# Experts' weights repeated by a transfer from memory and multiplied in by GpSimd, up sums in two banks

## The reference

```python
shared_out = _silu_and_mul(xf @ shared_w1.T) @ shared_w2.T
probs = jax.nn.softmax(xf @ gate_w.T, axis=-1)
routing_weights, selected = jax.lax.top_k(probs, TOP_K)
combine = zeros((T, E)).at[arange(T)[:, None], selected].add(routing_weights)
act = _silu_and_mul(gate_up)                 # silu(gate) * up, each expert's units
moe_out = jnp.einsum('te,tei,ehi->th', combine, act, w2)
return moe_out + shared_out
```

## Time and profile before

| | us |
|---|---|
| median of 3 runs | 1206.95 (1202.5 to 1208.85) |
| the profiled execution, its device time | 1210.45 |
| its span, first to last instruction | 1208.7 |
| TensorE busy with matmuls | 1041.3 |
| VectorE busy | 789.5 |
| ScalarE busy | 575.7 |
| GpSimd busy | 388.5 |
| TensorE's mean granted clock | 0.944 |

### The profile page before, as it was taken

One profiled execution on the slowest core, in us unless ns is written; L12 is line 12 of the kernel. 1 busy time (PEld: TensorE's weight loads), 2 busy tenths in 40 slices (PEclk: granted clock), 3 DMA queues, 4 the chain that ended last, 5 costly groups with the idle time before them and its releaser, 6 DMA issues. The chain is left out here.

```text
span 1208.7 us, 19206 instructions
## 1 busy us (share of the span) xinstructions
PE 1041.3 (86%) x6554; PEld 783.9 (65%) x6554; DVE 789.5 (65%) x1651; ACT 575.7 (48%) x1129; POOL 388.5 (32%) x423
## 2 busy tenths in 40 slices
PE   3699878999877898859999875799999889999998
PEld 3456536888766677736665454566655578888887
DVE  6367756577865466748888676677776365656655
ACT  3578753443433244306567542146555634444443
POOL 5312213355402244331211232222111044555553
PEclk9899979899998899969999997699999999999999
DMA  7957611342320127564550244937250122333332
GB/s 200 253 117 162 141 48 57 94 144 82 96 79 1 42 83 168 152 140 111 141 114 21 61 105 116 196 64 168 84 90 21 40 65 76 104 101 101 105 106 85
DMA packets 72762, 124.98 MB, mean 103 GB/s; under 512 B 9453, under 2 KB 41478, under 8 KB 70250
## 3 DMA queue, kind: packets, MB, share of 16 engines
q1 hardware_dynamic: 63274, 90.49, 24.6%
q0 software_dynamic: 9408, 33.45, 15.9%
HBM read 94.15 MB, written 30.80 MB: 103 GB/s over the span
## 5 line engine op out<-in xcount | busy, mean ns | idle before, releaser
L2008 DVE TENSOR_TENSOR ff_hl<-ff_h,ff_hh 128x512 fp32r<-128x512 f32 x114 | 135.4, 1188 | 154.2 <-ACT ff_hh L1894 153.8
L606 PE MATMUL psum<-ff_xh,ff_wh 128*128 128x512 f32 x424 | 175.9, 415 | 25.2 <-POOL ff_wl L1953 16.5
L1953 POOL TENSOR_TENSOR ff_wl<-ff_raw,ff_wh 128x512 fp32r<-128x512 f32 x92 | 119.8, 1302 | 236.7 <-ACT ff_wh L1905 236.7
L1050 ACT ACTIVATE probs<-psum 128x512 f32<-128x512 f32 x256 | 144.6, 597 | 85.1 <-PE psum L866 81.2
L1918 ACT ACTIVATE ff_s<-psum 128x512 f32<-128x512 f32 x98 | 58.6, 598 | 257.7 <-PE psum L606 248.2
L866 PE MATMUL psum<-queries,keys 128*128 128x512 f32 x384 | 156.9, 440 | 13.1 <-DMA keys<-keys_out 4.9
L606 PE MATMUL psum<-ff_xh,ff_wl 128*128 128x512 f32 x392 | 157.3, 401 | 0.0
L875 PE MATMUL psum<-keys,queries 128*128 128x512 f32 x256 | 118.4, 479 | 25.2 <-DMA queries<-queries_out 9.5
L606 PE MATMUL psum<-ff_wh,ff_hh 128*128 128x256 f32 x456 | 131.0, 291 | 9.2 <-DVE ff_hl L2008 9.2
L606 PE MATMUL psum<-ff_wh,ff_hl 128*128 128x256 f32 x456 | 130.1, 289 | 0.0
L899 PE MATMUL psum<-probs,values 128*32 128x256 f32 x1664 | 113.0, 394 | 2.0 <-DVE probs L1444 1.9
(11 more groups left out here) (268 smaller groups left out, 2194.0 us busy)
## 6 DMA issues: line engine op xcount, KB each, us to landing
ff_raw<-in_ff SPq DMA_DIRECT2D x92, 320.0 KB, 3.0
keys_out<-keys_turned SPq DMA_DIRECT2D x36, 512.0 KB, 4.2
keys<-keys_out POOLq DMA_DIRECT2D x48, 384.0 KB, 7.8
ff_raw<-in_ff SPq DMA_DIRECT2D x106, 128.0 KB, 2.1
queries_out<-queries_turned SPq DMA_DIRECT2D x36, 256.0 KB, 3.0
queries<-queries_out POOLq DMA_DIRECT2D x32, 256.0 KB, 4.8
w_raw<-in_w SPq DMA_DIRECT2D x12, 256.0 KB, 3.5
queries<-queries_out POOLq DMA_DIRECT2D x16, 192.0 KB, 7.7
```

The costliest lines, as they stand in the source:

```text
L606: last = eng.matmul(dst, lhs[i](k), rhs[j](k), start=start and n == 0, stop=stop and n == groups * len(pairs) - 1, skip_group_check=True)
L1050: ins = eng.activation(dst, src, ACT.Exp, scale=SCALE)
L1953: then(eng.tensor_tensor(ff_wl[:, slot, 0:2 * D], raw(n, slot)[:, 0:2 * D], ff_wh[:, slot, 0:2 * D].bitcast(F32), ALU.subtract), "f_w1r")
L2008: then(eng.tensor_tensor(ff_hl[:, slot, :], ff_h[:, slot, :], ff_hh[:, slot, :].bitcast(F32), ALU.subtract), "f_hr")
```

## The change

The select columns, the `combine` matmul and VectorE's `weighted` go. Instead, ScalarE copies the turned weights (experts by 512 tokens) to `combine` in f32 as one part; SP writes them to memory so that each run of 16 units has its own row (`weights_out`, two transfers for each half), and then loads, for each tile, its 8 rows with each row repeated on 16 partitions (`load_weights`, 256 KB) into a new buffer `ff_w`. GpSimd multiplies `silu(n)` by it (`weighted`), between `lo_up(n+1)` and `lo_down(n)`. VectorE's `gated(n)` multiplies that by the up sum and gives the hidden values at once. The bank set free serves as a second up bank, so that `up(n)` waits for `gated(n-2)`. In layer 1 the shared expert comes first, and its two tiles get a row of ones. ScalarE's order becomes `split_up(n+1)`, `half_hi(n-1)`, `silu(n)`, `split_down(n)`; `split_up(n+1)` waits for `up(n-1)` and handles 512 columns, and the `u` piece is 256 KB.

```diff
+RUN = 16
+RUNS = P // RUN
-GATE_BANKS, UP_BANK, SPREAD_BANK = (5, 6), 7, 4
+GATE_BANKS, UP_BANKS = (5, 6), (7, 4)
...
             def up(n, slot, h):
-                w(eng, "f_td", n)
+                w(eng, "f_hm", n - 1)
...
-            def spread(n, slot, h):
-                w(eng, "f_hm", n)
-                then(eng.matmul(psum[:, SPREAD_BANK, :], ff_wh[:, slot, BS:BS + P], combine[h][:, :], start=True, stop=True),
-                     "f_cf")
...
-                    w(eng, "f_cf", n - 1)
+                    w(eng, "f_uf", n - 1)
                     ins = eng.activation(ff_wh[:, slot, 0:BD], raw(n, slot)[:, 0:BD], ACT.Copy)
...
             def body(n, slot, some, j):
-                if not sign:
-                    silu(n, slot)
                 last = isinstance(n, int) and n == N - 1
                 if not last:
                     split_up(n + 1, 1 - slot, j + slot)
                 half_hi(n - 1, 1 - slot)
+                if not sign:
+                    silu(n, slot)
                 split_down(n, slot, j)
...
+            def weighted(n, slot, j):
+
+                eng.wait_ge(sems[f"d_fw{slot}"], (j + (ff_before(f, f"d_fw{slot}") + 1)) * 16)
+                w(eng, "f_sd", n + 1)
+                then(eng.tensor_tensor(ff_s[:, slot, :], ff_s[:, slot, :], ff_w[:, slot, :], ALU.mult), "f_sw")
...
                 if not (isinstance(n, int) and n == N - 1):
                     lo_up(n + 1, 1 - slot)
+                weighted(n, slot, j)
                 lo_down(n, slot)
...
             def gated(n, slot):
-                w(eng, "f_sd", n + 1)
+                w(eng, "f_sw", n + 1)
                 w(eng, "f_uf", n + 1)
-                then(eng.tensor_tensor(ff_s[:, slot, :], ff_s[:, slot, :], psum[:, UP_BANK, :], ALU.mult), "f_td")
-
-            def weighted(n, slot):
-                w(eng, "f_cf", n + 1)
-                w(eng, "f_td", n + 1)
                 w(eng, "f_hh", n - 1)
-                then(eng.tensor_tensor(ff_h[:, slot, :], ff_s[:, slot, :], psum[:, SPREAD_BANK, :], ALU.mult), "f_hm")
+                then(eng.tensor_tensor(ff_h[:, slot, :], ff_s[:, slot, :], psum[:, UP_BANKS[slot], :], ALU.mult), "f_hm")
...
+        def weights_out(eng, h):
+
+            spec, ends = FFN[f], RUNS * tiles
+            runs = wm[f][h].rearrange("t g c -> (t g) c")
+            e0, each = spec["HS"] // RUN if SHARED_FIRST[f] else 0, spec["H"] // RUN
+            e1 = e0 + spec["E"] * each
+            w(eng, "f_cth", h + 1)
+            src = combine[h][0:spec["E"], :].rearrange("e (one c) -> e one c", one=1)
+            eng.dma_start(runs[e0:e1, :].rearrange("(e g) c -> e g c", g=each),
+                          src.to_broadcast([spec["E"], each, HALF])).then_inc(sems["d_wm"], 16)
+            s0, s1 = (0, e0) if e0 else (e1, ends)
+            src = combine[h][spec["E"]:spec["E"] + 1, :].rearrange("e (one c) -> e one c", one=1)
+            eng.dma_start(runs[s0:s1, :].rearrange("(one g) c -> one g c", one=1),
+                          src.to_broadcast([1, s1 - s0, HALF])).then_inc(sems["d_wm"], 16)
+
+        def load_weights(eng, n, tile, slot, h):
+            w(eng, "f_sw", n - 1)
+            if isinstance(n, int) and SHARED_FIRST[f] and n % tiles < FFN[f]["HS"] // P:
+                eng.dma_start(ff_w[:, slot, :], a["one"].to_broadcast([P, HALF])).then_inc(sems[f"d_fw{slot}"], 16)
+                return
+            src = wm[f][h][bass.ds(tile, 1), :, :].rearrange("one g (r c) -> (one g) r c", r=1)
+            eng.dma_start(ff_w[:, slot, :], src.to_broadcast([RUNS, RUN, HALF])).then_inc(sems[f"d_fw{slot}"], 16)
...
         def sp(eng, first, last):
             def load(n, slot, some, _):
-                load_tile(eng, n, n - tiles * half_of(some), slot)
+                h = half_of(some)
+                load_tile(eng, n, n - tiles * h, slot)
+                if not sign:
+                    load_weights(eng, n, n - tiles * h, slot, h)
...
-            steps(step, max(first, tiles), last)
+            first = max(first, tiles)
+            if first == tiles <= last and not sign:
...
+                n = tiles + ones
+                load_tile(eng, n, ones, n % 2)
+                weights_out(eng, 1)
+                load_tile(eng, n + 1, ones + 1, (n + 1) % 2)
+                eng.wait_ge(sems["d_wm"], weights_written(f, 1))
+                for m in (n, n + 1):
+                    load_weights(eng, m, m - tiles, m % 2, 1)
+                first = n + 2
+            steps(step, first, last)
```

More of the change, by code:

```diff
@@ L368, in __init__ @@
                 else:
-                    self.before[st] = ("f_acc", 4) if ring == FIRST_SUMS else ("f_lo", 2 * KC) if blk == 3 else ("f_ctd", 2)
+                    self.before[st] = ("f_acc", 4) if ring == FIRST_SUMS else ("f_lo", 2 * KC) if blk == 3 else ("f_cth", 2)
                 kind, by = emptied(blk, st)
@@ L475, in flamingo @@
     down_row = at("down_row", OREG + 4096, [P, D])
-    combine = [at(f"combine{i}", (SREG + 8192, OREG + 4096)[i], [P, HALF], F32R) for i in range(2)]
+    combine = [at(f"combine{i}", (SREG + 8192, OREG + 4096)[i], [P, HALF]) for i in range(2)]
     ff_tensors = []
@@ L544, in flamingo @@
     nd = nc.dram_tensor("maxima_out", (B, HALVES, 64, P), F32, kind="Internal").ap()
+    wm = {f: [nc.dram_tensor(f"weights_out{f}{h}", (TILES[f], RUNS, HALF), F32, kind="Internal").ap() for h in range(2)]
+          for f in ROUTED}
     kept = nc.dram_tensor("kept", (KT, P), F32, kind="Internal").ap()
@@ L1087, in do @@
                 elif st[0] == "ce":
-                    ff_parts[blk].weights_hi(eng, 0, plan.bank["ct",])
+                    ff_parts[blk].weights(eng, 0, plan.bank["ct",])
                 if st in between:
@@ L1229, in ln @@
                     eng.wait_ge(sems[f"d_x{b}"], 16)
+                if blk:
+                    ff_wait(eng, blk - 1, "f_acc", QT * (b + 1))
                 for qt in range(QT):
@@ L1643, in clear @@
         def clear(self, eng):
-            eng.memset(combine[0][:, :].bitcast(F32), 0.0)
             eng.memset(rt_w[:, :, self.E:24], -1.0)
@@ L1668, in route @@
             if part == 0:
-                if h:
-                    eng.memset(combine[1][:, :].bitcast(F32), 0.0)
                 self.w(eng, "f_rt", h + 1)
@@ L1704, in turn_weights, with weights @@
             then(last, "f_ct")
-        def weights_hi(self, eng, h, bank):
+        def weights(self, eng, h, bank):
             self.w(eng, "f_ct", h + 1)
             then(eng.activation(combine[h][0:self.EC, :], psum[0:self.EC, bank, :], ACT.Copy), "f_cth")
-        def weights_lo(self, eng, h, bank):
-            EC = self.EC
-            self.w(eng, "f_cth", h + 1)
-            then(eng.tensor_tensor(combine[h][32:32 + EC, :], psum[0:EC, bank, :], combine[h][0:EC, :].bitcast(F32),
-                                   ALU.subtract), "f_ctd")
     ff_parts = [Part(f) for f in range(4)]
@@ L1863, in body @@
                     w(eng, "f_lo", 2 * KC)
-                    w(eng, "f_ctd", 2 if not sign else 0)
                 gate(n, slot, h)
@@ L1874, in body @@
                     up(n, slot, h)
-                    spread(n, slot, h)
             program(eng, body, does)
@@ L1921, in act @@
                     "route": lambda e, h, p: part.exponentials(e, h, B1) if p == 0 else None,
-                    "combine": lambda e, h: part.weights_hi(e, h, B2),
+                    "combine": lambda e, h: part.weights(e, h, B2),
                     "late": lambda e, *name: heads.late(*name), "lead": lambda e, n: lead.lead(n), "mem": lambda e, name: lead(name)}
@@ L2028, in dve @@
                     "route": lambda e, h, p: part.route(e, h, p, B1),
-                    "combine": lambda e, h: part.weights_lo(e, h, B2), "add": add,
+                    "add": add,
                     "late": lambda e, *name: heads.late(*name), "lead": lambda e, n: lead.lead(n), "mem": lambda e, name: lead(name)}
@@ L2039, in dve @@
                 gated(0, 0)
-                weighted(0, 0)
+                half_lo(0, 0)
                 gated(1, 1)
-                half_lo(0, 0)
-                weighted(1, 1)
             hooks.get(1, lambda: None)()
@@ L2077, in sp, with sp_weights @@
+        def sp_weights(eng):
+            if f != 1:
+                attention_over(eng, f, "o_full")
+            ones = 2 if SHARED_FIRST[f] else 0
+            for n in range(ones):
+                load_weights(eng, n, n, n % 2, 0)
+            weights_out(eng, 0)
+            eng.wait_ge(sems["d_wm"], weights_written(f, 0))
+            for n in range(ones, 4):
+                load_weights(eng, n, n, n % 2, 0)
         def sp(eng, first, last):
             def load(n, slot, some, _):
-                load_tile(eng, n, n - tiles * half_of(some), slot)
+                h = half_of(some)
+                load_tile(eng, n, n - tiles * h, slot)
+                if not sign:
+                    load_weights(eng, n, n - tiles * h, slot, h)
@@ L2081, in sp @@
```

(10 more changed lines are left out.)

50 lines of the change are left out of this document (26 added, 24 removed).

## The result

The changed kernel is slower: 1231.39 us median (1228.29 to 1235.44) against 1207.9 (1202.5 to 1210.54) for the kernel before, ratio 1.0203, 95% interval 1.0179 to 1.0227. Slower was the forecast's side, and 1231 lies in its range, but the rise is more than twice what the forecast's sum gives: 23.5 us between the medians, where the sum has 10. The profiled execution has a span of 1230.0 us, 21.3 more than before.

A forecast was written before the change was run, and what follows sets the result against it. TensorE was taken to bound layer 3 at 4.43 us per tile, the changed loop to take 4.80. Sum over tiles +10.8, small terms -1: +10 us, 1220 on the profiled execution, 1217 on the median; range 1192 to 1238.

The forecast's parts named there:

- Spread matmul, TensorE's step: 98 spread matmuls removed, 0.23 us of chain each, at most -22.5 us; TensorE's step becomes 4.20 us.
- The loop: From lo_down's end through SP's loads, split_up and GpSimd to lo_down again: 9.6 us per two tiles, 4.80 per tile.
- The landing: Gate-and-up piece's arrival, counted from E, the end of lo_down two tiles earlier: E+5.0, bounds E+3.7 and E+5.9.
- rival C: Repeated weights read uses half the DMA engines: landing after E+5.4, loop 10.0 to 10.5, 1230 to 1247 us; 0.18 with D.
- hand-overs: Two delays of 0.1 us each in the loop, one of them between the piece's landing and the next operation.
- Rival A: Weights transfer hidden, TensorE stays the bound: loop under 9.05 us, 1184 to 1200 us, as a point 1191; chance 0.22.
- Rival D: GpSimd's multiply costs more than lo_up: each +0.3 us adds 0.15 a tile, +8 us in all; 0.18 together with C.
- The shorter loop by issue order: half_lo, not GpSimd's multiply, held up at the shared port: 0.5 us off the loop, 4.55 instead of 4.80 per tile.
- Sum over tiles: Silu spacings shortened by 0.23, lengthened to the 9.6 loop: +0.6, -2.4, +12.7 us in layers 0, 1, 3; together +10.8.
- New waits: Waiting for the weights' write: layer starts 0, half changes +1.7 in layer 3, +0.5 each elsewhere; SP's other loads +2.
- banks: Second up bank, so up(1) no longer waits for gated(0): -1 us in layers 0 and 3, -1.5 in layer 1.
- the layers' ends: One of VectorE's two multiplies after the last up sum goes: -0.78 us in three layers, -2.3.

The follow-up runs named there:

- e1_run8: Changed kernel with each tile's weights written as 16 rows of 8 repeats instead of 8 of 16, doubling the write: 1235.26 us, ratio 1.0213.
- f1_write_doubled: Changed kernel with 16 rows written per tile but every second one read with 16 repeats, so only the write doubles: 1263.84 us, ratio 1.0475.
- e2: Changed kernel with SP issuing the next tile's gate-and-up piece ahead of the weights and the down piece: 1186.77 us, ratio 0.9816 to the kernel before.
- e3: Changed kernel without the per-tile weights transfers after the first two of each slot (computes something else): 1187.11 us, ratio 0.9810.
- e6: Changed kernel with the gate-and-up piece issued first and the multiply by the weights moved to VectorE: 1176.22 us, ratio 0.9760.
- b1_before_u_first: Kernel before the change, with SP issuing the next tile's gate-and-up piece ahead of the down piece: 1201.87 us, ratio 0.9965.
- g1_one_write: Changed kernel without the half changes' write and its wait; second halves read the first halves' weights (computes something else): 1228.50 us, ratio 1.0189.
- e5_u_first_run8: Changed kernel with the gate-and-up piece issued first and weights written as 16 rows of 8 repeats: 1211.47 us, ratio 1.0035.

## Where the prediction was right, and which of its terms failed

- **Spread matmul, TensorE's step.** Right: where TensorE is the bound the step is 4.16 to 4.20 (forecast 4.20).
- **The loop.** Right as a mechanism, and nearly so in size. The chain from `split_up` to `lo_down`'s end was forecast as 3.26 - 0.13 + 1.27 = 4.40 and measured 4.39. The exclusion of VectorE and GpSimd moved from `lo_down` (1.20 to 0.73) to the multiply (1.73 to 1.75 where `half_lo` overlaps, 1.27 alone) and was paid once. The landing was forecast at E+5.0 (bounds 3.7 and 5.9) and is E+5.3: 0.3 too low, and the reason is rival C's, the weights on half of the engines, which e1_run8 and f1_write_doubled show to be worth 0.6 to 0.75 us of the landing. Of the two hand-overs of 0.1 us the first was measured, the second not, and the loop came to 9.77 against 9.6. Layer 3's 35 steady spacings, without the half change, took 14.1 us more than before; 4.80 instead of 4.43 for each makes 13.0. The forecast's own way of summing over tiles, done with 9.77, gives +1.7, -1.9 and +16.4 us for layers 0, 1 and 3, together +16 in place of +10.8: by that estimate up to 5 us of what is missing hang on the landing.
- **Rival C.** Its mechanism, the weights on half of the engines, is what ran. Its loop of 10.0 to 10.5 was not reached, nor its own sign, a landing after E+5.4. That 1231 lies in its times (1230 to 1247), and that it lies in the forecast's range, is luck: the terms below made up the rest.
- **Rival A**, TensorE as the bound, is what e2, e3 and e6 give, 1176 to 1187, and not the kernel as changed. **Rival D** did not come: `lo_up` and the multiply cost the same alone.
- **The shorter loop by issue order**, 4.55 us a tile, did not come. In the stretch above `half_lo` starts at 1128.11, while `lo_up` runs, and ends at 1129.44; the multiply starts at 1128.86 and ends 1.15 us after it. What waited first got in first, as the forecast had assumed for this order.
- **What failed is the size of two terms of the sum**: the -2.4 (and +0.6) of "Sum over tiles" for layers 1 and 0, and "New waits" of 2.7 + 2. In the latter the 0 for layer 3's start was 1.8 us, and its half change holds 2.4 us beside the write, which alone was priced rightly. By layer, with the waits and banks as the forecast spread them (the 2 of SP's other loads halved between layers 0 and 1):

| | forecast | measured | missing |
|---|---|---|---|
| layer 0 | +0.6 - 1 + 0.5 + 1 = +1.1 | +3.9 | 3 |
| layer 1 | -2.4 - 1.5 + 0.5 + 1 = -2.4 | +7.6 | 10 |
| layer 3 | +12.7 - 1 + 1.7 = +13.4 | +17.6 | 4 |

**Layer 0.** Its 3 us are spread over several steps. The piece issued first takes 7.8 us back (146.7 to 138.9, e2_u_first), so the loop is in them as well; they were not taken apart further.

**Layer 1.** The forecast took its long steps (5 to 13 us) as cover for a loop of constant length. They are not: the piece's landing lengthens in the same steps, in which the next attention's key transfers run. In the kernel after, the pieces issued at 478.6 and 485.4 us land after 10.8 and 9.2 us, with key loads issued at 477 and 483, where 3 to 4 us are usual. ScalarE's waits for the piece in layer 1, 370 to 512 us, before, after and with the piece first:

```profile
ACT ff_wh L1905 <- DMA ff_raw<-in_ff: 5.1, 3, 2.8
```

```profile
ACT ff_wh L1900 <- DMA ff_raw<-in_ff: 41.8, 11, 7.6
```

```profile
ACT ff_wh L1900 <- DMA ff_raw<-in_ff: 14.9, 5, 5.6
```

The first of these, and the 7.2 us that b1_before_u_first gains in layer 1, say that the loop was at the surface there before the change. With the piece issued first layer 1 gets 9.3 us shorter (e2_u_first, 124.5 to 115.2). That is shown; that it is the keys' transfers which delay the piece is read from their place in the same steps and was not tried alone. Nor can it be all: of the 41.8 us some 14 lie before 440 us, where no keys move yet.

**Layer 3's rest.** The half change costs 13.65 us for two steps, 4.7 more than before; the forecast has 9.6 + 1.7, so 2.4 less. The write is not the missing part: it was priced at 1.7 and g1_one_write measures 1.8. Without it the pair still takes 11.9 us for 9.6, with two tiles' pieces ahead of their weights in SP's order; that this order is the cause was not tried alone. The start costs 9.21 against 7.45, where the forecast has nothing ("`gated(0)` was not early there: 0"): the write's way to memory and back, 9.7 us from issue to first multiply, ends after the `Silu` it was to run beside. f1_write_doubled and e5_u_first_run8 show the same wait growing to 11 us with the write.

The waits for the write are shown; how much of the 24 us between the medians each of these terms is worth by itself is known only as far as the spans above split it. The forecast's -2.3 for the layers' ends isn't told apart either: outside the three spans, and without the earlier first `Silu`, the profile has 1.7 us less.

## What to carry to other kernels

Before work is added to a tuned loop, close the loops that the bound engine hides: from the release of a buffer through the queue that refills it to the release again. Their slack (here 1.6 us in 8.85) is the budget, and a transfer put into a queue between the releasing wait and the next issue spends it at once; putting the issue that waits for less in front gave 45 us here. And a layer whose long steps look like cover needs its own look at the landing times in those steps: where its first reader has waited, there is no slack in that step.

## What the runs showed of the hardware

- A transfer that repeats rows costs SP more to issue: 0.64 us for 8 rows of 16 repeats and 0.56 for 16 rows of 8, against 0.33 for a plain piece. The forecast had 0.6 for the spacing of two issues, and the next piece went out 0.9 to 1.2 us after the weights.
- A write to memory that the next load waits for costs little less when it is small: from the end of its issue to that load 66 KB took 3.7 us, 400 KB 4.3, and 800 KB 9.4 and 10.2 (987.17 to 996.54 in f1_write_doubled, 975.12 to 985.36 in e1_run8). While 400 KB went out, the 16 DMA engines were 0.98 busy at 142 GB/s, where loads move at 229 to 262 GB/s with 0.84 to 0.87 busy (the rows of e1_run8 above): per engine and busy time about half. The rows are read again and again from 16 partitions; whether that or the write is the cause stays open.

```profile
973.00:974.00 1.00, 1.00 (x6) 0.83 (x5) 0.85 (x2) 0.60 (x1) 0.61 (x1) 1.00 0.98 142
```

- VectorE and GpSimd hold each other up in SBUF-only operations on whichever of them the multiply by the weights is put: on GpSimd it takes 1.27 us alone and 1.75 beside `half_lo`, on VectorE 0.68 alone and 1.22 beside `lo_down`.
- The same 10 us of the first attention had a granted clock of 0.66 in the profile before and 1.00 in the one after, and layer 0 began 6.2 us earlier; over all 13 profiles its first `Silu` lies between 172.2 and 180.7 us. Differences of a few us in one profile are read from spans that begin and end inside a stage.
